# Reordering the matmuls of a retention step: full-width work together, column-tiled work together

## What is computed

```python
q = (xf @ Wq.T).reshape(B, L, H, KD).transpose(0, 2, 1, 3)          # L = 1024, H = 8, KD = 32
k = (xf @ Wk.T * SCALING).reshape(B, L, H, KD).transpose(0, 2, 1, 3)
vr = (xf @ Wv.T).reshape(B, L, H, HD).transpose(0, 2, 1, 3)
qr = theta_shift(q, sin_q, cos_q)
kr = theta_shift(k, sin_k, cos_k)
qk = jnp.einsum('bhqd,bhkd->bhqk', qr, kr) * mask[None]
den = jnp.clip(jnp.abs(qk).sum(-1, keepdims=True), 1.0, 50000.0)
qk = qk / den
out = jnp.einsum('bhqk,bhkd->bhqd', qk, vr).transpose(0, 2, 1, 3)
# layer norm over each head, gelu, @ Wo.T, added to the input
```

## Time and profile before

| | |
|---|---|
| time, median of 3 runs | 2666.49 us (2666.29 to 2668.53) |
| span of the profiled execution | 2667.7 us |
| PE busy, whole span | 2586.6 us (97%) |
| DVE busy, whole span | 1844.4 us (69%) |
| ACT busy, whole span | 1459.4 us (55%) |
| POOL busy, whole span | 517.1 us (19%) |
| first and last scores of layer 0 | 41.5 us, 1142.7 us |

### The profile page before, as it was taken

One profiled execution on the slowest core, in us unless ns is written; L12 is line 12 of the kernel. 1 busy time (PEld: TensorE's weight loads), 2 busy tenths in 40 slices (PEclk: granted clock), 3 DMA queues, 4 the chain that ended last, 5 costly groups with the idle time before them and its releaser, 6 DMA issues. The chain is left out here.

```text
span 2667.7 us, 43895 instructions
## 1 busy us (share of the span) xinstructions
PE 2586.6 (97%) x15328; PEld 1732.6 (65%) x15328; DVE 1844.4 (69%) x2847; ACT 1459.4 (55%) x2044; POOL 517.1 (19%) x444
## 2 busy tenths in 40 slices
PE   5999999999999999969999969999999999999999
PEld 2333343333333434349999958888888888888888
DVE  3877777777777777747777658666666666666665
ACT  2665656565656565635666635555555555555554
POOL 2333333333333333211121210000000000000000
PEclk8999999999999999989999979999999999999999
DMA  6122222222232222121222224000000000000000
GB/s 230 47 77 58 76 68 59 80 55 82 56 84 57 77 58 68 48 85 64 95 94 75 98 90 143 25 25 24 24 24 24 24 24 24 24 24 24 24 17 16
DMA packets 116786, 157.95 MB, mean 59 GB/s; under 512 B 16272, under 2 KB 82328, under 8 KB 116384
## 3 DMA queue, kind: packets, MB, share of 16 engines
q1 hardware_dynamic: 116640, 156.01, 19.7%
HBM read 72.03 MB, written 33.59 MB: 40 GB/s over the span
## 5 line engine op out<-in xcount | busy, mean ns | idle before, releaser
L499 DVE TENSOR_TENSOR l_prod<-l_scores,l_window 128x1024 f32<-128x1024 f32 x512 | 624.0, 1220 | 211.4 <-PE l_scores L325 199.1
L690 ACT ACTIVATE l_absp<-l_prod 128x1024 f32<-128x1024 f32 x512 | 536.5, 1056 | 333.1 <-DVE l_prod L499 331.9
L1707 ACT ACTIVATE e_r<-e_h,e_bn,e_rs 128x512 f32<-128x512 f32 x512 | 399.0, 780 | 484.9 <-PE e_h L1558 480.7
L325 PE MATMUL l_scores<-l_qst,l_kst 96*128 96x512 f32 x1024 | 412.9, 484 | 15.4 <-DMA l_qst<-l_lo 11.6
L325 PEld LDWEIGHTS l_scores<-l_qst,l_kst 96*128 96x128 f32 x1024 | 168.1, 191 | 240.2 <-issue 180.2
L1558 PE MATMUL e_y<-e_whi,e_h2lo 128*128 128x256 f32 x1024 | 289.8, 283 | 0.0
L1557 PE MATMUL e_y<-e_wlo,e_h2hi 128*128 128x256 f32 x1024 | 289.7, 283 | 0.0
L1556 PE MATMUL e_y<-e_whi,e_h2hi 128*128 128x256 f32 x1024 | 289.2, 282 | 0.1
L339 PE MATMUL l_num<-l_prod,l_v 128*32 128x512 f32 x2048 | 273.5, 605 | 0.0
L350 PE MATMUL l_den<-l_absp,l_ones 128*32 128x512 f32 x2048 | 272.7, 604 | 0.0
L1802 DVE CAST e_h1hi<-e_r 128x512 fp32r<-128x512 f32 x256 | 111.2, 434 | 224.3 <-ACT e_r L1707 220.2
(11 more groups left out here) (191 smaller groups left out, 4447.0 us busy)
## 6 DMA issues: line engine op xcount, KB each, us to landing
l_kst<-l_hi SPq DMA_DIRECT2D x256, 64.0 KB, 2.0
l_qst<-l_hi SPq DMA_DIRECT2D x256, 64.0 KB, 2.0
l_raw<-in_xT SPq DMA_DIRECT2D x8, 1024.0 KB, 5.3
l_kst<-l_lo SPq DMA_DIRECT2D x128, 64.0 KB, 2.0
l_qst<-l_lo SPq DMA_DIRECT2D x128, 64.0 KB, 2.0
l_xo<-in_x SPq DMA_DIRECT2D x32, 256.0 KB, 2.8
x_scratch<-l_xo SPq DMA_DIRECT2D x32, 256.0 KB, 2.2
l_xr<-x_scratch SPq DMA_DIRECT2D x8, 1024.0 KB, 8.0
```

What stands on the lines that cost most here:

```text
L325: mm = nc.tensor.matmul(sc[j][:, s, :], kst[g][0:96, h, 128 * kt:128 * kt + 128], qst[c][0:96, h, :], start=True, stop=True)
L499: nc.vector.tensor_tensor(prod[n % 4][:], sc[j][:], win[:, 4 * g + 2 * j:4 * g + 2 * j + 2, w0:w0 + QC], ALU.mult).then_inc(prod_ready, 1)
L690: nc.scalar.activation(absp[n % 4][:], prod[n % 4][:], ACT.Abs).then_inc(abs_ready, 1)
L1707: nc.scalar.activation(r[m][:], p[m][:], ACT.Relu, bias=bn_[layer][1][:, m, e:e + 1], scale=rs[layer][:, m, e:e + 1]).then_inc(done, 1)
```

## The change

In each step PE now issues: scores half 0, part 0 of the side tasks, scores half 1, part 1 of the side tasks, then `sums`, then `weighted`. Before it was: scores half 0, `sums`, part 0, scores half 1, `weighted`, part 1. No instruction is added, taken out or resized; the semaphore each waits for and its count are the same; the other engines' programs are not touched. The tasks have been gathered into one function, called for each part (the body is cut here):

```diff
+                    def tasks(part):
+                        if kt == 0 and prep_q:
+                            A(f"q{p}", project, wq, g, c, part)
+                        if part == 0 and kt == 1 and post:
+                            Bk("nT" + tag, transpose_n, ph)
+                        if part == 1 and kt == 1 and post:
+                            A("dT" + tag, transpose_d, ph)
+                        if part == 1 and p == 2 and kt == 2 and not last:
+                            A("gn1", group_sums, mv[:, :, 0], agg_done, b + 2)
+                        if part == 1 and p == 2 and kt == 3 and not last:
+                            A("gn2", group_sums, gvar[:], gvar_ready, b + 2)
...
                     if more:
                         scores(nb, ni, 0)
+                    tasks(0)
+                    if more:
+                        scores(nb, ni, 1)
+                    tasks(1)
                     if i > 0:
                         sums(b, i - 1, first)
                     elif not first:
                         sums(b - 1, STEPS - 1, False)
-                    if kt == 0 and prep_q:
-                        A(f"q{p}", project, wq, g, c, 0)
...
-                    if more:
-                        scores(nb, ni, 1)
                     weighted(b, i, first)
-                    if kt == 0 and prep_q:
-                        A(f"q{p}", project, wq, g, c, 1)
...
```

More of the change, by code:

```diff
@@ L394, in body @@
                     more = i + 1 < STEPS or not last
+                    def tasks(part):
[9 more added lines that the diff above has]
+                            A("gn2", group_sums, gvar[:], gvar_ready, b + 2)
+                        if p != 2 and kt == 3 and prep_kv:
+                            A(f"k{p}", project, wk, (1 - p // 2), p % 2, part)
+                        if p == 2 and kt == 5 + (1 - part) and prep_kv:
+                            pe.wait_ge(xn_ready, 2 * b + 3 + (1 - part))
+                            A(f"k{p}", project, wk, (1 - p // 2), p % 2, 1 - part)
+                        if part == 0 and kt == 6 and post:
+                            Bk("zT" + tag, transpose_z, ph)
+                        if kt == 7 and p == 3:
+                            Bk("o0", out_proj, 0, 0, 4 * b + 3, part)
+                        if kt == 7 and prev and not first:
+                            Bk("o2'", out_proj, 1, 0, 4 * b, part)
+                        if kt == 4 and p == 0 and not first:
+                            Bk("o1'", out_proj, 0, 1, 4 * b - 1, part)
+                        if kt == 4 and p == 1 and not first:
+                            Bk("o3'", out_proj, 1, 1, 4 * b, part)
+                        if kt == (7 if p == 2 else 6) and prep_kv:
+                            A(f"v{p}", project_v, (1 - p // 2), p % 2, part)
                     if more:
                         scores(nb, ni, 0)
+                    tasks(0)
+                    if more:
+                        scores(nb, ni, 1)
+                    tasks(1)
                     if i > 0:
@@ L420, in body @@
-                    if kt == (7 if p == 2 else 6) and prep_kv:
-                        A(f"v{p}", project_v, (1 - p // 2), p % 2, 0)
-                    if more:
-                        scores(nb, ni, 1)
-                    weighted(b, i, first)
-                    if kt == 0 and prep_q:
-                        A(f"q{p}", project, wq, g, c, 1)
[L427 to L447, removed]
+                    weighted(b, i, first)
```

## The result

The changed kernel takes 2623.4 us (median of 4 runs, 2622.1 to 2625.2), against 2667.5 us for the kernel before beside it. The ratio is 0.9833, with a 95% interval of 0.9819 to 0.9847. That is 44 us less, where 85 were forecast, and 2623.4 us lies above the stated range, which ended at 2614. The profiled execution spans 2622.4 us, 45.3 less than before.

The account below looks back on a forecast made before the run. PE was taken to bound the retention stage, losing time at tiling changes; 95.6 - 10.7 + 1.8 - 1.5 = 85.2 us off the profiled 2667.7 gave 2582.5, so a median of 2581 us, range 2568 to 2614.

Parts of the forecast that it names:

- No wait is new, but two stand elsewhere: Reordered step: only scores half 1 and the side tasks wait elsewhere; a plain step keeps 0.19 us in hand.
- the merged quadruple: Four scores in a row on PE at full clock: 1.09 us, against 1.34 for two pairs.
- What bounds the kernel: Retention stage: PE sets the pace, busy 1078.0 of 1080 us, with 0.76 us of each 3.32 us step outside column time.
- the cost of a tiling change: Group boundaries on PE, four a step: scores and column-tiled groups each run 0.12 to 0.13 us over a column time.
- (b): Only drains are saved; each scores pair keeps its 0.12 us entry, gain 0.25 us a step, 2613 us; chance 0.10.
- The size of the merged step: Plain step on PE: 2.94 us in place of 3.32, gain taken as 0.375 us in 255 steps, 95.6 us.
- No stall in phases 0, 1 and 3: Small DVE work between products in steps 2, 3 and 6 is covered by PE's side tasks; no stall counted.
- Moved past queues: ACT starts k2 about 1.4 us later; heads' transposes stay covered by little, else phase 3 pays up to 1 us a batch.
- (a): DVE late in every phase, not only phase 2: 48 us lost in place of 10.7, 2619 us; chance 0.14.
- The walk through phase 2: PE waits 0.27, 0.72 and 0.53 us in steps 3 to 5; 1.5 us in 7 batches, 10.7 us.
- The first microseconds and POOL's cover: First batch's DMA wait costs four steps' gain, 1.5 us; transposes of POOL's scaled heads stay covered, by little.
- (c): The cost belongs to a group's first matmul whatever the tiling, so nothing is saved: 2670 us; chance 0.04.
- (d): Chain of scores half 1, second product and next half 1 becomes the step: slower, 2700 us; chance 0.04.

Follow-up runs that it names:

- k2 early: Changed kernel with ACT making the high part of k2 before taking the den bank in step 0 of phase 3; 2614.1 us.
- the first sum late: Changed kernel with only the first group sum, in step 2 of phase 2, moved behind num; 2616.8 us.
- the three repairs: Changed kernel with each batch's last step in the old order, phase 2's first group sum behind num, and k2's high part before taking the den bank; 2607.1 us.
- part 1 late: Changed kernel with part 1 of the side tasks moved behind num in every step; 2610.2 us.
- the old last step: Changed kernel with only step 31 of each batch in the old order, with four tiling changes; 2609.5 us.

## Why the prediction was wrong, point by point

The step that failed first is "No wait is new, but two stand elsewhere". Three more covers moved with the tasks, and none was walked: that of the branch at the loop's edge (11 us), that of the den transposes of phase 3 (9.6 us), and that of the first group sum. The other step is a term of the sum, the merged quadruple, 0.04 us a step too short (10 us). The points in order:

**What bounds the kernel; the cost of a tiling change.** Right. The boundaries were where the time went, and the merged groups have no gap at their inner boundary. Rival (b), and with it the Trainium skill's sentence that a weight load overlaps matmuls in flight only where the row group differs (TensorE: Matmul & The Clock Gate, Part 3, The mechanism), would put 0.3 us between the second and third scores. The timeline of PE has the third and the fourth of the quadruple of 565.48 here:

```profile
566.05 0.40 PE L325 MATMUL l_scores<-l_qst,l_kst 96*128 96x512 f32 x1
...
566.28 0.40 PE L325 MATMUL l_scores<-l_qst,l_kst 96*128 96x512 f32 x1
```

With 0.34 us to the second (565.82), the third follows 0.23 us after it. The trace doesn't agree with the rule.

**The size of the merged step.** A term was mis-sized: 2.98 us for 2.94. The inner distance of scores is 0.235 us at the full clock (medians 0.235 and 0.233), not the 0.213 of its columns. I had scaled a bare 0.427 us of the half clock. A row at the full clock was to be had in the trace of before, from the experts, whose matmuls of this length follow one another at 0.23 us:

```profile
1790.08 0.39 PE L1556 MATMUL e_h<-e_h1hi,e_whi 128*128 128x512 f32 x1
1790.31 0.39 PE L1557 MATMUL e_h<-e_h1lo,e_whi 128*128 128x512 f32 x1
```

255 x 0.04 = 10 us.

**No stall in phases 0, 1 and 3.** Wrong for phase 3, 9.6 us. "Moved past queues" had ACT starting k2 some 1.4 us later, and the DMAs and POOL behind it; it left out DVE: `q_rotate_in` waits for `lo_ready` and holds the bank of the den transposes, which had moved ahead of den and num. The run with k2 early shows the whole chain. The covers in steps 2, 3 and 6 held, and rival (a) didn't come.

**The walk through phase 2.** Right in what it had, wrong in what it left out. With the first group sum put late, its three waits measure 0.34, 0.61 and 0.6 us, where it says 0.27, 0.72 and 0.53. But the first sum waits through `a_free` for DVE's `take_den`, a wait that the old order covered with den and num. It was not walked. In the changed kernel it takes the place of the first two walked waits, so neither the wait of scores in step 3 nor that of `gn2` for L552, two of the signs given, is there. It adds little by itself: 1.9 us a batch in place of 1.5, 13 us in all against 10.7. The other 5 us of the 18.0 are three half-clock stretches behind it.

**The first microseconds and POOL's cover.** The 1.5 us that were given up at the first batch's DMA were mostly not lost: the scores that wait for it start at 56.99 us, 1.2 us earlier than in rows 12. The transposes of the scaled heads never waited.

**What the prediction doesn't have at all.** The loop's edge, 11 us more than before; the row was in the trace of before, as 0.3 us of idle "issue" at 599.34 us, and read as harmless. And the granted clock: four stretches at the half level, 1.5 us each, which lie within the edge's and phase 2's sums (one and three). I checked that the clock was full, and not what the new waits would do to it.

**The sum.** 10 us for the pitch, 11 for the edge, 9.5 for phase 3, 7 for phase 2 over the forecast (5 of them the clock), and about 3 net over the other steps: 40 us, which is what the profiled execution lacks (85.2 - 45.3).

**Range and rivals.** (a) and (b), at 2619 and 2613, came nearer to the measured time than the forecast, by mechanisms that aren't in the trace. (c) and (d) are out. The range's upper end rested on half of (a); two separate surprises of 10 us each weren't in it.

## What to carry to other kernels

A reordering that saves the engine time moves every wait of the tasks it moves: list each moved task's semaphores, the bank it overwrites included, and walk each back to its producer through the other engines, not only the wait of the main loop. Tasks of the same tiling can stand on either side of the tiled groups, so put those that wait at the end of the step, where the wait of the next step's work is no later. A wait that you take away can uncover the next one, as at the two group sums, so read what is left and not only the time. Then look at the last step ahead of a branch back: what is queued there hides the branch, and a merge that shortens it is paid in full. How long a branch takes has to be read in each version, of all loops.

## What the runs showed of the hardware

- The branch back of PE's retention loop takes the sequencer 3.3 to 4.3 us, in each version; it costs what isn't covered by queued matmuls (0.1 to 0.3 us before, 1.9 to 2.7 after, five times). Those of the two other loops take 0.21 to 0.24 us, but with six bodies written out ahead of it that of the experts' loop takes 3.6 to 3.9 us. The length of the body alone doesn't decide: the experts' body has some 1590 entries of PE in the trace at 0.21 us, the retention body 1761. What does stays open.
- The granted clock went to half for some 3.4 us behind idle times of 0.61 us (the version with the first sum late, and the three repairs), 1.2 us (the changed kernel) and 1.9 to 2.7 us (the loop's edge), but not behind each: the changed kernel has edges of 2.6 and 2.7 us, the version with part 1 late waits of 0.9 to 1.2 us, and the version with the old last step seven waits of 1.1 to 1.2 us, without such a stretch. What tells them apart stays open.
- A 96x512 matmul on the split (fp32r) operands follows another at 0.235 us at the full clock and at 0.42 us at the half clock, so it doesn't halve with the clock. A round of four float32 matmuls over 512 columns in column tiles takes 0.43 us at the full clock (the second round of the num group of 564.51 starts at 564.94), two times 0.213. Why the two forms differ wasn't tried.
